# GNN with two message-passing layers: the segment sums of layer 0 go over run sums made on VectorE, and the node products are turned

## What is computed

```python
h = jnp.maximum(_layernorm(x, axis=-1), 0.0)
# layer 0
agg = jax.ops.segment_sum(h[src], dst, num_segments=N_NODES)
x = x + (agg @ W_rel.T + b_rel + h @ W_root.T)
h = jnp.maximum(_layernorm(x, axis=-1), 0.0)
# layer 1
edge_weights = jax.nn.silu(edge_features @ We1 + be1) @ We2 + be2
agg = jax.ops.segment_sum(h[src] * edge_weights, dst, num_segments=N_NODES)
x = x + (jax.nn.silu(agg @ Wn1 + bn1) @ Wn2 + bn2)
```

## Time and profile before

| | us |
|---|---|
| median of 3 runs | 4755.86 (4752.82 to 4757.91) |
| profiled execution | 4776.76 |
| its span, first to last instruction | 4774.7 |
| mean granted TensorE clock, as a share of full speed | 0.700 |
| last gather of layer 0 starts at | 2316.00 |
| busy: TensorE / its weight loads | 2496.3 / 1646.9 |
| busy: GpSimd / VectorE / ScalarE | 2967.1 / 1005.3 / 704.4 |

### The profile page before, as it was taken

One profiled execution on the slowest core, in us unless ns is written; L12 is line 12 of the kernel. 1 busy time (PEld: TensorE's weight loads), 2 busy tenths in 40 slices (PEclk: granted clock), 3 DMA queues, 4 the chain that ended last, 5 costly groups with the idle time before them and its releaser, 6 DMA issues.

```text
span 4774.7 us, 34714 instructions
## 1 busy us (share of the span) xinstructions
PE 2496.3 (52%) x10150; PEld 1646.9 (34%) x10150; DVE 1005.3 (21%) x1790; ACT 704.4 (15%) x1212; POOL 2967.1 (62%) x3135
## 2 busy tenths in 40 slices
PE   1332322323232322233347777777776777777778
PEld 0232322222232322232224444444443444434444
DVE  2511111111111111111312222222222222222223
ACT  2400000000000000000112222222222222212222
POOL 5366666666666666666466666666666666666663
PEclk9765655555555655655668777877777877877878
DMA  4212222212222222212212222222222222222222
GB/s 131 67 52 54 52 55 56 54 51 56 54 56 54 53 54 55 54 51 56 64 53 70 65 63 65 68 65 70 66 66 62 69 65 70 66 63 68 66 65 62
DMA packets 230577, 296.69 MB, mean 62 GB/s; under 512 B 68707, under 2 KB 160277, under 8 KB 230432
## 3 DMA queue, kind: packets, MB, share of 16 engines
q0 software_dynamic: 100096, 205.20, 16.6%
q10 hardware_dynamic: 61378, 60.59, 4.6%
q1 hardware_dynamic: 69086, 30.73, 2.4%
HBM read 269.81 MB, written 26.48 MB: 62 GB/s over the span
## 4 chain that ended last, share of the span: by engine, by line
another core or an unknown queue 44%; PE 28%; issue 17%; DVE 6%; DVEq 2%; ACT 1%; POOL 0%; DMA 0%; ACTq 0%; SPq 0%; POOLq 0%
PE seg L377 10%; PE hid_b L419 3%; PE hid_a L424 3%; DVE onehot L744 3%; PE ew_a L377 2%; PE hid_c L424 2%; PE ew_b L430 2%; PE hid_b L424 2%; PE ew_a L430 1%; DVEq L752 1%; PE hid_a L419 1%; PE hid_c L419 1%; DVE agg L756 1%; DVE e_stats L658 1%
## 5 line engine op out<-in xcount | busy, mean ns | idle before, releaser
L324 POOL DMA_INDIRECT rows<-h_rows,idx x3060 | 2902.0, 948 | 1723.0 <-issue 946.8
L377 PE MATMUL seg<-onehot,rows 128*128 128x128 f32 x4784 | 884.3, 340 | 1347.0 <-DVE onehot L744 523.8
L377 PEld LDWEIGHTS seg<-onehot,rows 128*128 128x128 f32 x4784 | 802.1, 250 | 1460.5 <-issue 1038.9
L377 PE MATMUL ew_a<-onehot,rows 128*128 128x128 f32 x1472 | 289.0, 324 | 574.3 <-issue 529.2
L744 DVE TENSOR_TENSOR onehot<-iota_ps,dst_rel 128x1536 f32<-128x1536 f32 (+1 forms) x278 | 461.0, 1658 | 0.8 <-DVE dst_rel L732 0.6
L377 PEld LDWEIGHTS ew_a<-onehot,rows 128*128 128x128 f32 x1472 | 246.6, 235 | 570.5 <-issue 566.5
L852 DVE TENSOR_TENSOR rows<-ew_a,rows 128x512 f32<-128x512 f32 x207 | 142.8, 690 | 1110.6 <-remote 636.3
L756 DVE TENSOR_TENSOR agg<-seg,agg 128x128 f32 x207 | 60.4, 292 | 1179.3 <-remote 1110.5
L424 PE MATMUL hid_c<-hidden,we_sb 128*128 128x512 f32 x230 | 149.4, 735 | 161.6 <-ACT hidden L601 160.4
L852 DVE TENSOR_TENSOR rows<-ew_b,rows 128x512 f32<-128x512 f32 x184 | 126.7, 689 | 507.2 <-PE ew_b L430 173.2
L424 PE MATMUL hid_a<-hidden,we_sb 128*128 128x512 f32 x278 | 219.6, 882 | 0.0
(11 more groups left out here) (134 smaller groups left out, 1851.1 us busy)
## 6 DMA issues: line engine op xcount, KB each, us to landing
rows<-h_rows,idx POOLq DMA_INDIRECT x3060
ef_a<-ef_blocks ACTq DMA_DIRECT2D x70, 300.0 KB
node_work<-ef_blocks ACTq DMA_DIRECT2D x47, 300.0 KB
xs<-x SPq DMA_DIRECT2D x40, 256.0 KB
ys<-y_rows SPq DMA_DIRECT2D x26, 256.0 KB
out<-xs ACTq DMA_DIRECT2D x26, 256.0 KB
y_rows<-ys ACTq DMA_DIRECT2D x25, 256.0 KB
h_rows<-node_work ACTq DMA_DIRECT2D x23, 256.0 KB
```

The lines of the kernel that those rows point to most:

```text
L324: pool.indirect_dma_start(out=rows[:, u, t, :], out_offset=None, in_=table, in_offset=bass.IndirectOffsetOnAxis(ap=idx[:, j:j + 1], axis=0 ...
L377: mm = pe.matmul(seg[layer][g % 2][:, 0:P], rows[:, u, t, :], onehot[:, g % 2, k * TB + t, :], start=(k == 0 and t == 0), stop=(last and t ...
```

## The change

**Layout.** The host reorders the edges inside each group. Before, consecutive edges lay in consecutive partitions of a tile. Now each partition holds the 12 (in the last group 8) consecutive edges of the group, one per tile. As edges are sorted by target, a partition holds a few runs of equal targets.

**Layer 0, run sums.** In each group and for each of R = 3 runs VectorE multiplies the gathered rows with a mask that keeps the edges of run r, into a PSUM tile `wide` of three banks (128x1536), and reduces over the tiles to one row per partition (`run_sums`). Each operation waits for the one before. TensorE then needs 3 matmuls a group, one for each run, with a one-hot of the runs' targets. The sums rotate over three PSUM banks and are added two groups later (LAG = 2). GpSimd's wait before it gathers a group again is now for VectorE's third multiply (`s_pick`). Masks are made once an iteration, one-hots twice, and all six window starts are loaded at once.

```diff
-                    hold(pool, s_seg[layer], i * G + (g + 1))
+                    if layer == 0:
+                        hold(pool, s_pick[R - 1], i * G + (g + 1))
+                    else:
+                        hold(pool, s_seg[1], i * G + (g + 1))
...
-            def segment_sum(layer, i, u):
+            def run_sums(i, g):
+                pe.wait_ge(s_sum[R - 1], i * G + (G + g + 2))
+                for r in range(R):
+                    mm = pe.matmul(run_seg[g % 3][:, 0:P], run_sum[g % SUM_BUFS][:, r, :], run_hot[g][:, r, :],
+                                   start=(r == 0), stop=(r == R - 1))
+                mm.then_inc(s_seg[0], 1)
+
+            def segment_sum(i, u):
                 g, k = u // GB, u % GB
-                if layer == 1 and k == 0:
+                if k == 0:
                     pe.wait_ge(s_acc[1], i * G + (g + 1))
                 last = u == blocks_of(g)[-1]
                 for t in range(TB):
-                    mm = pe.matmul(seg[layer][g % 2][:, 0:P], rows[:, u, t, :], onehot[:, g % 2, k * TB + t, :],
+                    mm = pe.matmul(seg_ps[:, 0:P], rows[:, u, t, :], onehot[:, g % 2, k * TB + t, :],
                                    start=(k == 0 and t == 0), stop=(last and t == TB - 1))
                 if last:
-                    mm.then_inc(s_seg[layer], 1)
+                    mm.then_inc(s_seg[1], 1)
...
-                        segment_sum(0, p * ITERS, u)
+                    run_sums(p * ITERS, g)
...
                     steps = node_update0(p * (ITERS - 1) + it - 1, 0)
                     for g in range(G):
                         if g in steps:
                             steps[g]()
-                        pe.wait_ge(s_onehot, i * G + p + (g + 1))
-                        pe.wait_ge(s_rows[0][g], landed(i, g))
-                        for u in blocks_of(g):
-                            segment_sum(0, i, u)
-            hold(pe, s_acc[0], passes * N_SUMS + 1)
+                        run_sums(i, g)
```

```diff
+            def next_turn(n):
+
+                v.tensor_scalar(run_first[:, :], run_first[:, :], float(R), None, ALU.add).then_inc(s_pass, 1)
+                dve.wait_ge(s_pass, n + 1)
+                v.tensor_tensor(run_wrap[:, :], run_first[:, :], run_last[:, :], ALU.is_gt).then_inc(s_pass, 1)
+                dve.wait_ge(s_pass, n + 2)
+                v.tensor_scalar(base_step[:, :], run_wrap[:, :], float(P), None, ALU.mult)
+                v.tensor_scalar(run_wrap[:, :], run_wrap[:, :], -1.0, 1.0, ALU.mult, ALU.add).then_inc(s_pass, 1)
+                dve.wait_ge(s_pass, n + 3)
+                v.tensor_tensor(run_first[:, :], run_first[:, :], run_wrap[:, :], ALU.mult)
+                v.tensor_tensor(base_off[:, :], base_off[:, :], base_step[:, :], ALU.add)
+                v.tensor_scalar(base_row[:, :], base_row[:, :], base_step[0:1, 0:1], float(BASE_MAX), ALU.add,
+                                ALU.min).then_inc(s_pass, 1)
+                dve.wait_ge(s_pass, n + 4)
+                v.tensor_scalar(run_now, iota_f[:, 0:R], run_first[:, 0:1], None, ALU.add).then_inc(s_pass, 1)
+                dve.wait_ge(s_pass, n + 5)
+                run_targets(n + 5)
```

```diff
                 def product():
                     pe.wait_ge(s_nT, n + 1)
+                    pe.matmul(node_t[r][:, :], w_root_sb[:, :], hT[r], start=True, stop=False)
+                    pe.matmul(node_t[r][:, :], w_rel_sb[:, :], aggT[r], start=False, stop=True).then_inc(s_np, 1)
+
+                def turned_back():
+                    pe.wait_ge(s_nbias, n + 1)
                     for t in range(TB):
-                        o = node_o[r][:, t * D:(t + 1) * D]
-                        pe.matmul(o, hT[r][:, t * P:(t + 1) * P], w_root_sb[:, :], start=True, stop=False)
-                        mm = pe.matmul(o, aggT[r][:, t * P:(t + 1) * P], w_rel_sb[:, :], start=False, stop=True)
-                    mm.then_inc(s_no, 1)
-                return {1: product}
-
-            with pe.Fori(0, passes) as p:
+                        tr = pe.transpose(node_o[r][:, t * D:(t + 1) * D], aggT[r][:, t * P:(t + 1) * P], ident[:, :])
+                    tr.then_inc(s_no, 1)
+                return {2: product, 3: turned_back}
+
+            with pe.Fori(0, passes0) as p:
...
+                    pe.matmul(node_t[r][:, :], wn2_sb[:, :], hT[r], start=True, stop=True).then_inc(s_mp, 1)
+
+                def turned_back():
+                    pe.wait_ge(s_mbias, n + 1)
                     for t in range(TB):
-                        mm = pe.matmul(node_o[r][:, t * D:(t + 1) * D], hT[r][:, t * P:(t + 1) * P], wn2_sb[:, :],
-                                       start=True, stop=True)
-                    mm.then_inc(s_mo, 1)
-                return {4: hidden_layer, 7: product}
+                        tr = pe.transpose(node_o[r][:, t * D:(t + 1) * D], hT[r][:, t * P:(t + 1) * P], ident[:, :])
+                    tr.then_inc(s_mo, 1)
+                return {4: hidden_layer, 7: product, 9: turned_back}
...
+                def bias():
+                    act.wait_ge(s_np, n + 1)
+                    nc.scalar.activation(aggT[r], node_t[r][:, :], ACT.Identity, bias=b_rel_col[:, :]).then_inc(s_nbias, 1)
+
...
-                return {0: turned, 1: lambda: node_std(n, r), 2: h1, 3: y, 4: stored}
-
-            with act.Fori(0, passes) as p:
+                return {0: turned, 1: bias, 2: lambda: node_std(n, r), 3: h1, 4: y, 5: stored}
```

More of the change, by code:

```diff
@@ L28 @@
 HALF = 9
+HALF_G = 3
 GB = 3
+R = 3
+MAX_RUNS = GB * TB
+LAG = 2
+SUM_BUFS = 3
 G = -(-U // GB)
@@ L356, in _ @@
             pe.wait_ge(s_ident, 1)
+            pe.wait_ge(s_run, 1)
+            pe.matmul(node[:, 0:P], scratch[:, 0:P], ident[:, :], start=True, stop=True).then_inc(s_run_max, 1)
             with pe.Fori(0, GROUPS // H_SETS) as k:
@@ L670, in shift_of @@
                                        ALU.mult, ALU.mult).then_inc(s_done, 1)
+            dve.wait_ge(s_dst, 16)
+            dst_flat = dst_sb[:, :, :].rearrange("p k t -> p (k t)")
+            by_group = run_of.rearrange("p (i e) -> p i e", e=U * TB)[:, :, bass.ds(0, G, step=GB * TB)]
+            keep_start = scratch.rearrange("p (i e) -> p i e", e=U * TB)[:, :, bass.ds(0, G, step=GB * TB)]
+            v.tensor_scalar(dst_flat, dst_flat, 1.0, None, ALU.add)
+            v.memset(scratch, 1.0).then_inc(s_setup, 1)
@@ new lines, in _ @@
+            dve.wait_ge(s_setup, 2)
+            v.tensor_tensor(run_of[:, 1:N_BLOCKS * TB], dst_flat[:, 1:N_BLOCKS * TB], dst_flat[:, 0:N_BLOCKS * TB - 1],
+                            ALU.not_equal)
+            v.memset(keep_start, 0.0).then_inc(s_setup, 1)
+            dve.wait_ge(s_setup, 3)
+            v.memset(by_group, 0.0).then_inc(s_setup, 1)
+            dve.wait_ge(s_setup, 4)
+            v.tensor_tensor_scan(run_of, scratch, run_of, 0.0, ALU.mult, ALU.add).then_inc(s_setup, 1)
+            dve.wait_ge(s_setup, 5)
@@ L749, in one_hot, with masks @@
                     ALU.is_equal)
[L751 to L756 removed]
+            def masks(it):
+                v.tensor_tensor(run_mask,
+                                dst_rel[:, bass.ds(it * U, U), :].rearrange("p k t -> p (k t)")
+                                .unsqueeze(1).to_broadcast([P, R, U * TB]),
+                                run_now.unsqueeze(2).to_broadcast([P, R, U * TB]),
+                                ALU.is_equal).then_inc(s_mask, 1)
@@ new lines, in add_runs, with window_bases @@
+            def add_runs(g, base, value):
+                window = agg[0][:, bass.ds(base, P)]
+                dve.wait_ge(s_seg[0], value)
+                v.tensor_tensor(window, run_seg[g % 3][:, 0:P], window, ALU.add).then_inc(s_acc[0], 1)
+            def window_bases(first, count):
+                return nc.values_load_multi_w_load_instructions(
+                    base_row[0:1, bass.ds(first, count)], engines=(mybir.EngineType.DVE,), min_val=0, max_val=BASE_MAX,
+                    skip_runtime_bounds_check_because="base_row holds node numbers clamped to BASE_MAX")[1]
@@ L758, in edge_stats, with window_base, add_window @@
+            def window_base(it, g):
+                return window_bases(it * G + g, 1)[0]
+            def add_window(i, it, g):
+                base = window_base(it, g)
+                window = agg[1][:, bass.ds(base, P)]
+                dve.wait_ge(s_acc[1], i * G + (g + 1))
+                dve.wait_ge(s_seg[1], summed(i, g))
+                v.tensor_tensor(window, seg_ps[:, 0:P], window, ALU.add).then_inc(s_acc[1], 1)
             def edge_stats(p, u):
@@ L806, in _ @@
                 hold(dve, s_hcopy[r], GROUPS // H_SETS + 1)
-            with dve.Fori(0, passes) as p:
-                one_hot(0, 0).then_inc(s_onehot, 1)
+            with dve.Fori(0, passes0) as p:
+                masks(0)
+                one_hots(0, 0)
+                one_hots(0, 1)
                 edge_stats(p, 0)
@@ L909 @@
     ef_pad[:N_EDGES] = edge_attr_50
```

(10 more changed lines are left out.)

303 lines of the change are left out of this document (188 added, 115 removed).

## The result

The changed kernel takes 4859.03 us (median of 4 runs, 4850.34 to 4863.81) against 4754.34 for the kernel before beside it (4 runs). The ratio is 1.023, 95% interval 1.0213 to 1.0246. The forecast was 4646, its range 4520 to 4840.

What follows compares the result with a forecast made beforehand. Layer 0 was taken as bound by gathers plus pauses for TensorE's held-back updates; 2 + 25 - 178 + 22 + 6 + 2 + 7 + 4 = -110 us from 4755.86 gave 4646 us, range 4520 to 4840.

Steps and rivals of the forecast that it cites:

- What bounds the kernel: Layer 0: 68 gathers at 1.25 us, 85.0 us, plus two pauses, 12.6 us, make the 97.46 us iteration.
- the pace: Layer 0, TensorE: held back, a matmul starts every 1.93 us, so 48 rows take 93 us against 85.0 of gathers.
- one pause an iteration is ample: Layer 0: one GpSimd pause, which let 71 matmuls through before, suffices for TensorE to catch up; two pauses before.
- The pause: Layer 0, GpSimd: 6.1 to 6.5 us beyond the ordinary 0.3, taken as 4 an iteration, giving T = 89 us.
- Rival three: Layer 0: held-back updates keep two pauses, period 93 to 97.5 us, one-time costs full, 4760 to 4860 us; chance 0.15.
- The chain rival: Layer 0, VectorE: 36 hand-offs cost about 1.1 us each, period about 106 us, total about 5030 us; chance 0.16.
- The multiplies don't block gathers: Layer 0: multiplies with masks in PSUM take no lock; the rival that they block, over 5200 us, got chance 0.03.
- VectorE's cost: Layer 0: 1.75 us per full-group operation, 0.12 us per hand-off to itself, 72 us an iteration against 14.6 before.
- Iteration 0: First layer-0 iteration: LayerNorm plus 68 us of run sums on VectorE, about 105 us against 85 of gathers; +25 us.
- Between the layers: Last layer-0 gather to first of layer 1: VectorE hanging back +22, further-turn table +6, last updates +2 us.
- Setup: Before the gathers restart: run detection and tables go in front of the h loop, which starts later; +2 us.
- layer 1: Layer 1: long product and transposes on TensorE, bias copy on ScalarE; +7 us over 23 iterations, +4 at the end.

Runs made afterwards that it cites:

- run sums with late `x1`: Changed kernel with both layers' node products as before the change and VectorE's add of x moved behind group 5: 4956.41 us, 1.037 of before with late updates.
- run sums alone: Changed kernel with both layers' node products as before the change: 4874.54 us, 1.0192 of before with late updates; 4044.67 us, 1.0113 without.

## Why the prediction was wrong

- **What bounds the kernel** was read rightly: gathers plus the pauses that TensorE's late updates force. The quiet batches confirm it from the other side: without late updates the layer-0 iteration of every version is 85 us, the 68 x 1.25 of the prediction.
- **The step that failed is the pace**, "at the held-back step that is 48 x 1.93 = 93 us", hence "one pause an iteration is ample". The 1.93 was the distance between starts of matmuls; what VectorE waits for is the update, and once updates are behind it takes 2.7 us a row. At that pace 44 rows are 119 us (six sums at 16.1, a product and the transposes at 11.1 each), against 85 of gathers. The updates fall behind by 32 to 36 us in the second iteration of each pattern, until a pause.
- **The pause was mis-sized with it**: 6.1 to 6.5 taken from the earlier trace rows, 4 us an iteration after allowing for iterations without one. There is one in every second iteration, so the number of pauses was even overestimated, but each is 30.1 us: 85.0 + 29.8 / 2 = 99.9, the measured period. 18.4 of it is the update, so the pause doesn't free it at once as the prediction had it; 11.7 is VectorE's chain up to the third multiply, which the change has put between TensorE and GpSimd. Before, GpSimd restarted 0.6 us after VectorE saw the update.
- **Rival three** (held-back updates keep two pauses, 4760 to 4860) had the cause, held-back updates, and its upper end is the time, 4859; that it fits so closely is luck. The period is 99.9 where it had 93 to 97.5, and the one-time costs (setup, iteration 0, between the layers, layer 1) are 44 us together, where it had 98. Its picture of two short pauses was wrong. It got 0.15. The prediction said that VectorE's add "stops VectorE, and through it GpSimd", and then priced the stop by the old pause.
- **The chain rival** is refuted: multiplies and reductions follow each other every 1.8 us deep inside a run of gathers (1341.28, 1343.08). The multiplies don't block gathers, as said; 85 us an iteration in quiet batches with 18 of them shows it.
- **VectorE's cost** was right for each operation (1.76 for 1.75) and for the sum; a hand-off to itself costs 0.04 us (1341.28 + 1.76 to 1343.08), not 0.12.
- **Iteration 0:** +25 was forecast. The time from the gathers' restart to iteration 2's first gather changed by -2.0 us (94.6 to 92.6). That VectorE's added work lay in its waits there is likely, not shown.
- **Between the layers** +30, measured +43.8: VectorE hangs back by +40.4 where 22 was taken and 53 was the bound; the table and the updates cost 3.4 where 8 was taken. **Setup** and **layer 1** were within 7 us. The setup term holds in a late batch alone: in a quiet one the gathers restart 31.7 us later with the run sums than without.

By the ledger, 34.4 + 43.8 + 4.6 - 2.4 = +80.4 us between the profiled executions.

The cause of the lateness itself stays open, and so does why batches differ. That the pace goes by rows rests on intervals of 6, 4 and 10 rows within one kernel, and it can't be the price of a row in general: the kernel before passes 152 rows in 97.46 us. Nor is it in force soon after a restart. In run sums with late `x1`, where gathers run unbroken from 1203.38 on, TensorE starts a sum of 6 rows, a product of 16 and a sum of 6, and VectorE adds that last sum 39.4 us after the first started, at most 1.4 us a row:

```profile
1215.29 1.65 PE L405 MATMUL ew_a<-onehot 128*128 128x128 f32 x6 [9.19 <-DVE onehot L894]
```

```profile
1254.70 0.29 DVE L901 TENSOR_TENSOR agg<-ew_b,agg 128x128 f32 x1 [5.69 <-issue]
```

The run that would have changed the rows a group had no late batch, so what sets TensorE's pace was tested from VectorE's side only. None of the versions beat the kernel before by more than the measurement tells; a version without VectorE's chain between update and gather wasn't tried.

## What to carry to other kernels

When an engine's updates arrive late, measure the distance between the consumers' operations that wait for them, not between the producer's starts: the first is the rate at which work is passed on. Here TensorE's rows were cut to under a third (152 to 44), and even with VectorE's work cut as well the period stayed at 96.7 to 97.4 us, where it had been. Whatever is put between a late update and the engine that must restart (here 11.7 us, from `x1` to the third multiply) is paid at each pause. A pause's length read from one program is a price of that program's chain, not of the chip.

## What was not expected of the hardware

**Late updates come and go with the batch.** The kernel before on the chip numbered 7 took 4000 us in one batch and 4788 and 4807 in two others; run sums alone issued 802 gathers in a 1000 us window in a quiet batch and 689 in a late one. A fifth of the time depends on it, far more than on any edit here.

**Operations with two SBUF inputs do hold up gathers.** In the setup of the changed kernel, VectorE and then GpSimd:

```profile
39.01 1.83 DVE L760 SCALAR_TENSOR_TENSOR onehot<-dst_rel,consts_ps,dst_sb 128x1564 f32<-128x1564 f32 x1
...
42.76 1.85 DVE L760 SCALAR_TENSOR_TENSOR onehot<-dst_rel,consts_ps,dst_sb 128x1564 f32<-128x1564 f32 x1
```

```profile
38.18 0.94 POOL L354 DMA_INDIRECT rows<-x,idx  x1 [0.30 <-issue]
39.43 2.24 POOL L354 DMA_INDIRECT rows<-x,idx  x1 [0.30 <-issue]
41.97 0.94 POOL L354 DMA_INDIRECT rows<-x,idx  x1 [0.30 <-issue]
43.22 2.21 POOL L354 DMA_INDIRECT rows<-x,idx  x1 [0.30 <-issue]
```

A gather that starts while such an operation runs takes 2.2 us instead of 0.94. The short add of xs and node_work, both in SBUF, does it too when it starts first; VectorE and GpSimd again:

```profile
1132.90 0.68 DVE L963 TENSOR_TENSOR ys<-xs,node_work 128x512 f32<-128x512 f32 x1
```

```profile
1133.06 1.34 POOL L354 DMA_INDIRECT rows<-h_rows,idx  x1 [0.30 <-issue]
```

Between 160 and 2350 us nine gathers take 1.25 to 1.43 us, and each starts 0.06 to 0.25 us after this add. Where the gather started 0.23 to 0.46 us before the add, it took 0.94 or 0.95. The multiplies of 1.76 us with the mask in PSUM lengthen none. The Trainium skill ("SBUF — State Buffer", Who interferes with whom) says that a VectorE instruction with two SBUF inputs contends with a GpSimd instruction that reads SBUF, and that issue order decides which of them blocks; the gather reads its indices from `idx` in SBUF, and the trace agrees. So the prediction's "VectorE doesn't slow the gathers here" held for one moment: in the kernel before add and gather start within 0.02 us of each other in all 21 cases (1026.08 and 1026.09 in the earlier trace rows), and the gather stays at 0.94 or 0.95.

In the setup six gathers of iteration 0 are lengthened, by 8.3 us together, and the last of them starts 8.2 us later than before (87.44 to 95.67). In the late batch the wait behind them hid it.
